# Two attentions that run all key groups over one half of the rows, then over the other

## What is computed

```
x = x + attn0(layernorm(x), ctx, ctx, mask)     # rope on q and k, softmax, @ wo
x = x + ffn0(layernorm(x))                      # 512 -> 1376 -> 512, rounded to int8 steps
x = x + attn1(layernorm(x), concat(ctx, x))     # rms norm on q and k, softmax, @ Wo
x = x + ffn1(layernorm(x))                      # int8 fake quantisation, two 512 x 512 products
```

## Time and profile before

| | us |
|---|---|
| median of three runs | 1549.08 |
| the three runs | 1549.51, 1549.08, 1546.22 |
| the profiled execution, its own time | 1546.81 |
| span from its first to its last instruction | 1545.0 |

### The profile page before, as it was taken

The page is one execution under the profiler, slowest core; times in us unless marked ns, Lnnn a source line. Parts: engine busy times, 40 slices in busy tenths (PEclk is TensorE's granted clock), DMA queues, the critical chain, the costliest instruction groups (busy, mean ns, idle before and its releaser), DMA issues.

```text
span 1545.0 us, 28746 instructions
## 1 busy us (share of the span) xinstructions
PE 1481.8 (96%) x11536; PEld 1271.7 (82%) x11536; DVE 957.9 (62%) x1989; ACT 591.7 (38%) x1428; POOL 565.1 (37%) x468
## 2 busy tenths in 40 slices
PE   6899999999999998999899999999999999999985
PEld 5788888888888876887698899888889988888973
DVE  7655666666656667666866556455655645565588
ACT  4322132222213214442355353444435344443556
POOL 4535363444436324552134122222312222231248
PEclk9999999999999999999999999999999999999999
DMA  6111020101102003220102011010101001010201
GB/s 196 36 34 43 28 69 22 49 28 42 42 28 62 8 21 96 61 77 21 42 28 70 1 42 29 28 42 17 54 2 42 28 28 42 15 55 1 82 2 55
DMA packets 84302, 64.45 MB, mean 42 GB/s; under 512 B 7280, under 2 KB 71024, under 8 KB 84176
## 3 DMA queue, kind: packets, MB, share of 16 engines
q1 hardware_dynamic: 83600, 62.47, 14.0%
q10 hardware_dynamic: 576, 0.20, 0.0%
HBM read 60.56 MB, written 2.10 MB: 41 GB/s over the span
## 4 chain that ended last, share of the span: by engine, by line
PE 47%; DVE 2%; POOL 1%; issue 1%; ACT 0%; DVEq 0%; ACTq 0%; POOLq 0%
PE att_proj L70 35%; PE att_att L788 4%; PE att_sco L746 4%; PE att_att L763 2%; PE att_proj L710 1%; PE att_sco L725 1%; POOL ffn_y L468 0%; DVE ffn_top L420 0%; DVE ffn_y L462 0%; POOL x_rows L406 0%; DVE ffn_y L416 0%; PE att_att L234 0%; DVE stats L375 0%; DVE x_rows L1031 0%; ACT ffn_y L427 0%
## 5 line engine op out<-in xcount | busy, mean ns | idle before, releaser
L144 POOL TENSOR_TENSOR att_w_lo<-w_raw,att_w_hi 128x512 fp32r<-128x512 f32 x160 | 203.4, 1295 | 209.4 <-ACT att_w_hi L139 203.5
L1380 POOL TENSOR_TENSOR att_probs<-att_probs,att_total 128x512 f32<-128x512 f32 x64 | 82.8, 1294 | 461.4 <-DVE att_total L1015 344.9
L70 PE MATMUL att_proj<-att_w_hi,kv_hi 128*128 128x256 f32 x768 | 221.0, 288 | 10.7 <-DVE kv_lo L252 10.5
L70 PE MATMUL att_proj<-att_w_lo,kv_hi 128*128 128x256 f32 x768 | 216.3, 282 | 0.0
L70 PE MATMUL att_proj<-att_w_hi,kv_lo 128*128 128x256 f32 x768 | 216.1, 281 | 0.0
L70 PE MATMUL att_proj<-att_w_hi,att_o_hi 128*128 128x512 f32 x512 | 206.7, 404 | 5.1 <-issue 4.6
L70 PE MATMUL att_proj<-kv_hi,att_w_hi 128*128 128x512 f32 x512 | 208.9, 408 | 1.5 <-DVE kv_lo L243 1.5
L70 PE MATMUL att_proj<-kv_hi,att_w_lo 128*128 128x512 f32 x512 | 202.7, 396 | 0.0
L70 PE MATMUL att_proj<-kv_lo,att_w_hi 128*128 128x512 f32 x512 | 202.7, 396 | 0.0
L1031 DVE TENSOR_TENSOR x_rows<-att_proj,x_rows 128x512 f32<-128x512 f32 x128 | 88.4, 691 | 183.8 <-PE att_proj L70 183.7
L70 PE MATMUL att_proj<-att_w_lo,att_o_hi 128*128 128x512 f32 x512 | 201.6, 394 | 0.0
(11 more groups left out here) (165 smaller groups left out, 2855.4 us busy)
## 6 DMA issues: line engine op xcount, KB each, us to landing
w_raw<-in_wq SPq DMA_DIRECT2D x64, 256.0 KB, 3.0
w_raw<-in_wo SPq DMA_DIRECT2D x64, 256.0 KB, 2.8
w_raw<-in_wk SPq DMA_DIRECT2D x16, 256.0 KB, 3.3
w_raw<-in_wv SPq DMA_DIRECT2D x16, 256.0 KB, 3.2
w_raw<-in_gate_t SPq DMA_DIRECT2D x10, 256.0 KB, 3.0
w_raw<-in_up_t SPq DMA_DIRECT2D x10, 256.0 KB, 3.1
w_raw<-in_down_t SPq DMA_DIRECT2D x10, 256.0 KB, 3.0
spare<-in_ctx_t SPq DMA_DIRECT2D x4, 512.0 KB, 5.7
```

The lines of the kernel that those rows point to most:

```text
L70: ins = eng.matmul(out, a, b, start=(first and n == 0), stop=(last and n == 3 * len(terms) - 1))
L144: eng.tensor_tensor(self.lo[:, chunk], self.raw[:, n % RAW_SLOTS], raw(self.hi[:, chunk]), ALU.subtract)\
L1380: eng.tensor_tensor(probs[:, u % 2, 0:n], probs[:, u % 2, 0:n], total[:, u % 2, 0:n].unsqueeze(2).broadcast_to([P, n, KL]), ALU.mult)\
```

## The change

The order of the units is turned round. VISITS lists (g, h) with the half outside: all eight groups over rows 0 to 511, then all eight over rows 512 to 1023. A unit is now u = 2v + n, with visit v and head pair n. Each visit needs its ten chunks, so each chunk is loaded, rounded and split twice. The fillers become: visit 0's two units make the keys of visit 1; after that n = 0 projects the visit before, n = 1 makes the next visit's keys.

The late half is needed from visit 8 on. Its statistics move behind unit 1 of DVE (first attention), its row scales behind unit 2. One late tile each is normalised on DVE at the end of units 3, 5, 7 and 9, and transposed, rounded and split as an extra projection job in units 4, 6, 8 and 10 (LATE_X). The late context goes through the ring of raw slots, as four entries "ctx" of turns, in unit 5 (visit 2, LATE_CTX). The last visit's output chunks go into the query chunks' place.

```diff
+VISITS = [(g, h) for h in range(HALF) for g in range(NKV)]
+LATE_CTX = 2
+LATE_X = {4: 4, 6: 5, 8: 6, 10: 7}
...
-        for g in range(NKV):
-            self.turns += [(g, C_O + i) for i in range(GROUP)]
-            if g + 1 < NKV:
-                self.turns += [(g + 1, c) for c in (C_Q, C_Q + 1, C_K, C_V, C_Q + 2, C_Q + 3)]
+        self.turns += [(1, c) for c in (C_K, C_V, C_Q, C_Q + 1)]
+        for v in range(len(VISITS)):
+            if v + 1 < len(VISITS):
+                self.turns += [(v + 1, c) for c in ((C_K, C_V) if v else ()) + (C_Q + 2, C_Q + 3)]
+            if v + 1 < len(VISITS):
+                self.turns += [(v, C_O + i) for i in range(GROUP)]
+            if v + 2 == len(VISITS):
+                self.turns += [(v + 1, C_O + i) for i in range(GROUP)]
+            if v == LATE_CTX:
+                self.turns += [("ctx", k) for k in range(KT)]
+            if v + 2 < len(VISITS):
+                self.turns += [(v + 2, C_Q), (v + 2, C_Q + 1)]
...
+        if visit == "ctx":
+            src = self.ctx[:, chunk, BANK:2 * BANK]
...
-        if g == 0 and n < 2:
-            return keys(0, 1)[KVH // 2 * n:KVH // 2 * (n + 1)]
+        if v == 0:
+            return keys(1)[KVH // 2 * n:KVH // 2 * (n + 1)]
         if n == 0:
-            return outs(g - 1, 1)
...
+            return [("out", v - 1, t) for t in range(4)]
+        return keys(v + 1) if v + 1 < len(VISITS) else []
...
                 fill_rest(work)
+                if u in LATE_X:
+                    x_job(LATE_X[u])
                 q_job(u + 2, 0)
...
+                if u in LATE_X:
+                    lower_late(LATE_X[u])
                 q_refine(u + 1)
                 take_q(u + 2, 0)
                 take_q(u + 2, 1)
                 out_low(u)
...
+                if u == 1 and rope:
+                    for t in range(4, NT):
+                        first_stats(t)
+                if u == 2:
+                    scale_rows(eng, st, chain, intake.stage, 1)
+                if u + 1 in LATE_X:
+                    normalise_late(LATE_X[u + 1])
...
-                if n == 2:
-                    round_w(g + 1, C_K, C_V, C_Q + 2, C_Q + 3)
+                if n == 0 and v < LAST:
+                    round_w(v + 1, *((C_K, C_V) if v else ()), C_Q + 2, C_Q + 3)
+                if n == 1:
+                    round_w(v, *range(C_O, C_O + GROUP))
+                if n == 1 and v == LATE_CTX:
+                    round_w("ctx", *range(KT))
+                if u in LATE_X:
+                    round_late(LATE_X[u])
                 copy_turned(u)
...
+                if n == 1 and v + 2 <= LAST:
+                    round_w(v + 2, C_Q, C_Q + 1)
+                if u == UNITS - 3:
+                    eng.wait_ge(proj_full, proj_job["q", UNITS - 1, 1] + 1)
+                    round_w(LAST, *range(C_O, C_O + GROUP))
...
+                if n == 0 and 0 < v < LAST:
+                    split_w(v + 1, C_K, C_V)
+                if n == 1:
+                    split_w(v, *range(C_O, C_O + GROUP))
                 rotate("q", u + 2, 0)
...
                 rotate("q", u + 2, 1)
...
+                if n == 1 and v == LATE_CTX:
+                    split_w("ctx", *range(KT))
+                if n == 1 and v + 2 <= LAST:
+                    split_w(v + 2, C_Q, C_Q + 1)
```

More of the change, by code:

```diff
@@ L220, in normalise @@
                           ALU.subtract, ALU.mult).then_inc(self.xn_done[t // 4], 1)
-    def normalise_late(self, eng, t):
-        st, ring = self.st, len(self.xn)
-        eng.wait_ge(st.rows_scaled, HALF * self.stage + t // 4 + 1)
-        need(eng, self.turned, t - ring + 1)
-        eng.activation(self.xn[t % ring], st.x[:, t], ACT.Identity, bias=st.shift[:, t:t + 1], scale=st.rstd[:, t:t + 1])\
-           .then_inc(self.xn_done[t // 4], 1)
     def turn(self, eng, t):
@@ L529, in attention @@
     for u in range(UNITS):
-        g, n = divmod(u, 4)
-        for i, what in enumerate(filling(g, n)):
+        for i, what in enumerate(filling(u)):
             number(*what)
@@ L543, in attention @@
             number("row", 0)
-        number("out", NKV - 1, 1, t)
+        number("out", LAST, t)
     if tail:
@@ L712, in q_sums, with x_job, turn_keys @@
                 last.then_inc(proj_full, 1)
-            def turn_keys(g, h):
-                need(eng, sco_drained, SJ * key_unit(g, h))
-                if g == 0 and h == 0:
+            def x_job(t):
+                job = proj_job["x", t]
+                eng.wait_ge(intake.xn_done[1], t - 3)
+                room(eng, job)
+                for k in range(KT):
+                    last = eng.transpose(proj[job % 4][:, k * P:(k + 1) * P], xn_late[:, k * P:(k + 1) * P], st.ident[:])
+                last.then_inc(proj_full, 1)
+            def turn_keys(v):
+                need(eng, sco_drained, SJ * 2 * v)
+                if v == 0:
                     eng.wait_ge(intake.x_split, 4)
@@ L839, in _ @@
                     intake.turn(eng, t)
-                for j in range(3):
-                    kv_job(0, 0, j)
-                intake.turn(eng, 4)
-                intake.turn(eng, 5)
-                kv_job(0, 0, 3)
+                for j in range(KVH):
+                    kv_job(0, j)
                 q_job(0, 0)
-                intake.turn(eng, 6)
-                intake.turn(eng, 7)
                 q_job(0, 1)
-                turn_keys(0, 0)
+                turn_keys(0)
                 q_job(1, 0)
@@ L1026, in out_low, with add_out @@
                        .then_inc(out_drained, 1)
-            def add_out(g, h, t):
-                job, row = proj_job["out", g, h, t], 4 * h + t
+            def add_out(v, t):
+                g, h = VISITS[v]
+                job, row = proj_job["out", v, t], 4 * h + t
                 eng.wait_ge(proj_full, job + 1)
@@ L1063, in _ @@
                     intake.lower_x(eng, t)
-                for t in range(4, NT):
-                    first_stats(t)
                 eng.wait_ge(tables_landed, 64)
                 for j in range(KVH):
-                    take(("kv", 0, 0, j))
-                scale_rows(eng, st, chain, 0, 1)
+                    take(("kv", 0, j))
                 take_q(0, 0)
@@ L1072, in _ @@
                 take_q(1, 0)
-                for t in range(4, NT):
-                    intake.lower_x(eng, t)
                 eng.wait_ge(mask_landed, 32)
@@ L1177, in _, with round_w, copy_v @@
         def _(eng):
-            def round_w(g, *chunks):
-                if g == NKV:
-                    return
+            def round_w(v, *chunks):
                 for chunk in chunks:
-                    weights.round_chunk(eng, weights.turn_of[g, chunk])
-            def copy_v(g, h, j):
-                job, half, pair = proj_job["kv", g, h, j], 2 * g + h, tile_of(h, j)
+                    weights.round_chunk(eng, weights.turn_of[v, chunk])
+            def copy_v(half, j):
+                job, pair = proj_job["kv", half, j], tile_of(half % 2, j)
                 bank = proj[job % 4][:].rearrange("p (b w d) -> p b w d", b=2, w=2)
@@ L1408, in _ @@
                 intake.lower_ctx(eng, 3)
-                eng.wait_ge(st.rows_scaled, 6)
-                split_w(0, C_Q, C_Q + 1)
-                split_w(0, C_Q + 2, C_Q + 3)
-                scale_keys(0, 0)
-                for t in range(4, NT):
-                    intake.lower_ctx(eng, t)
+                split_w(0, *range(C_Q, C_Q + GROUP))
+                scale_keys(0)
+                split_w(1, C_K, C_V)
+                split_w(1, C_Q, C_Q + 1)
             for u in range(UNITS - 2):
-                g, n = divmod(u, 4)
-                work = [what for what in filling(g, n) if what[0] == "kv"]
+                v, n = divmod(u, 2)
+                work = [what for what in filling(u) if what[0] == "kv"]
                 for what in work[:-1]:
@@ L1761, in build @@
         st.consts, st.qk_ready = st.sem("consts"), st.sem("qk_ready")
-        st.ctx_landed = [st.sem(f"ctx_landed{i}") for i in range(4)]
+        st.ctx_landed = [st.sem(f"ctx_landed{i}") for i in range(2)]
         st.ctx_cols = a["ctx_t"].rearrange("(k p) t -> p k t", p=P)
```

371 lines of the change are left out of this document (172 added, 199 removed).

## The result

The changed kernel takes **1598.95 us** (median of 4 runs, 1596.32 to 1601.33) against 1548.28 us for the kernel before (4 runs), a ratio of 1.033 with a 95% interval of 1.0316 to 1.0344. The forecast was 1556 us with a range of 1542 to 1565. The direction was right. The size was not: about 9 us were forecast and 50 came.

The account below looks back on a forecast made before the run. PE, busy 96% of the span, was taken as the bound. Terms -6.0 - 3.2 - 0.7 + 2.0 + 4.9 + 8.9 + 3.0 = +8.9 gave 1555.7, or 1558.0 from the median; forecast 1556 us, range 1542 to 1565.

Parts of the forecast that it names:

- So the doubled streaming costs nothing: Both attentions: 80 more chunks each to load, round and split stay beside PE, within covers of 0.3 to 2 us.
- theory B: Follow-up expectation, second attention: POOL's later splits or weight loads come too late for PE's projections; early refinement leaves 1595 to 1601.
- by the slack of rows 6 and 7 nothing does: Doubled splits holding up DVE on PE's path: 128 us by the port-lock rule at 0.8 us each, nothing by profiled slack.
- Rival 2: POOL crowded in each of 14 later keys units, 1.1 us lost per unit: +15, so 1571; chance 0.08.
- Start of the first attention: Late transposes leave the start, units 0 and 1 wait less: net 6.4 us gained, 6.0 taken.
- The seven small waits: First attention, seven units' PE waits for POOL's normalisation, some 0.46 us each, go: 3.2 us gained.
- Row scales: Moved to the end of DVE's unit 2, delaying unit 3: 1.7 us lost in first attention, 0.3 in second.
- Late context: Unit 5: ACT's context rounding waits for ring and DMA, PE idles 4.9 us in first attention, 8.9 in second.
- 1.5 + 1.5 for the clock: Lower clock behind each of the two unit 5 stalls: 3.0 us lost together, bounds 0 and 5.
- End of the first attention: Idle of 2.75 us before the projection at 566.37 shrinks as that half no longer ends there: 0.7 us gained.
- Second attention, transposes that come back: Late transposes leave the second attention's start and come back in later units, 1.6 us each way: net 0.
- Last visit: Output chunks use the query slots, unit 30's exponentials come some 3 us later: cost 0, bound 1.

Follow-up runs that it names:

- the early chain: Changed kernel with VectorE's ten dependent query-scale refinement instructions moved, in the second attention, from each unit's end to just behind q_means: 1561.12 us.
- the pieces: Changed kernel with each of POOL's output splits in the second attention cut into four instructions of 128 columns, VectorE's order unchanged: 1564.87 us.
- the chain last: Changed kernel with VectorE's query-scale refinement moved, in the second attention, behind the query-product copies and output remainder, last in its unit: 1564.26 us.
- the kernel before with the early chain: Kernel before the change, with VectorE's query-scale refinement moved to just behind q_means in the second attention: 1551.80 us, ratio 1.0029.
- the last kernel but one: Changed kernel, refinement early except second attention's units 0 and 1, context rounding behind output rounding, first attention's row scales inside unit 2: 1541.14 us.

## Why the forecast failed

**The step that failed is "So the doubled streaming costs nothing".** It was argued with care for what PE wants of POOL (the normalisation, the splits themselves) and of ScalarE (four more roundings), and those covers held: theory B fell, and the thirteen other keys units from 3 to 29 lost nothing. What the step left out is VectorE. It placed the four output splits of the second attention at 914.28 to 919.3, "ahead of the projection", and did not ask what VectorE does in just that stretch. It runs the chain. The trace of before had the sign. In its unit 5 two links of the chain took 1.02 and 0.96 us beside the key scaling of the earlier trace rows and the other eight 0.17. In its unit 6, where four splits run, three links took 1.2 us each (VectorE, then POOL):

```profile
932.12 1.21 DVE L164 TENSOR_TENSOR att_q_tmp<-att_q_rms 128x8 f32<-128x8 f32 x1
933.36 1.20 DVE L165 SCALAR_TENSOR_TENSOR att_q_tmp<-att_q_tmp,att_q_mean 128x8 f32<-128x8 f32 x1
934.60 1.23 DVE L166 SCALAR_TENSOR_TENSOR att_q_rms<-att_q_tmp,att_q_rms 128x8 f32<-128x8 f32 x1
```

```profile
930.77 5.03 POOL L144 TENSOR_TENSOR att_w_lo<-w_raw,att_w_hi 128x512 fp32r<-128x512 f32 x4
```

That chain took 5.2 us and PE didn't wait, so no list of waits showed it. In the keys units of the changed kernel mostly five or six splits follow the key scaling, and the chain starts with the scaling: some 7 us more than 2, with the two things that PE's projections need queued behind. The term is 0 in the sum and measured 37.1 us (by the medians of the runs: 37.8 with the early chain, 34.1 with the pieces).

**The sentence "by the slack of rows 6 and 7 nothing does"** is the same error. The rule beside it was the right one: the Trainium skill (SBUF — State Buffer, section SBUF: two separate sides) gives the lock between VectorE and POOL for the whole instruction. It also says, which I left out, that VectorE takes part in it only in a two-port mode or with two SBUF inputs. The trace agrees: L984 and L1040, with an operand in a bank, keep their 0.69 us, and the links with two SBUF inputs are held up. L188 has a single input, in SBUF, and was held up too (0.66 us with the chain last); in which mode it ran no run shows. I took 0.8 us per split from the earlier trace rows, one instruction held up once. A dependent chain is held up once for each link: the links start 1.23 us apart beside splits of 1.24 us (6.21 for five), so each arrives when the next POOL instruction has begun.

**Rival 2** (POOL crowded in every keys unit) came nearest, but it looked for POOL being late, in the first attention, and priced 1.1 us a unit. POOL was in time and made VectorE late, in the second.

The other terms, one by one:

- Start of the first attention: -6.0 with unit 2 at -8.0 before the transposes come back. Measured -7.3 at unit 2. PE waits 1.3 us in unit 0 (forecast 1.4), and the clock behind it is 1.00 where it was 0.79. The transposes come back with 2.0 us (forecast 1.6). Right.
- The seven small waits, -3.2: the units 9, 13 and so on to 29 take 14.52 us instead of 15.15, 0.6 us less each in six units; the seventh wait, of unit 5, is covered by the stall. Right.
- Row scales, 1.7 + 0.3: unit 3 of the first attention is 1.4 us longer (1.19 of it a wait for the normalisation), that of the second not at all. Right within the bounds.
- Late context, 4.9 + 8.9, with 1.5 + 1.5 for the clock: unit 5 is 5.3 and 9.95 us longer and unit 6 of the first attention loses 1.3 us at clock 0.77. The run that moved the rounding gave 15.3 us for all of it, forecast 16.8. Right, and by the mechanism described. Only where PE meets it in the second attention is another place: the wait of 8.02 us stands at the weighting, not at the next scores:

```profile
914.58 2.19 ACT L154 ACTIVATE att_w_hi<-w_raw 128x512 fp32r<-128x512 f32 x4
924.31 0.63 ACT L154 ACTIVATE kv_hi<-w_raw 128x512 fp32r<-128x512 f32 x1 [7.54 <-DMA w_raw<-in_ctx_t]
...
928.64 1.06 ACT L1257 ACTIVATE att_probs_t<-att_att 128x512 f32<-128x512 f32 x2
```

These are ScalarE's rows of unit 5 in the second attention: it stands 7.54 us for the context, and the copy of the turned probabilities, for which PE waits 8.02 us, stands behind it.

- End of the first attention, -0.7: the idle of the earlier trace rows is now 2.12 us instead of 2.75. Right.
- At unit 31 of the first attention the terms summed to -1.1, and -1.1 was measured. From there to the second attention's first scores the changed kernel lost 1.75 us (236.81 against 235.07) where -0.7, and -1.6 for the second attention's transposes that leave, were forecast. The clock differs: 0.95 in this stretch, 0.97 before. At equal clock the new order is the shorter one: at 0.95 the kernel before with the early chain took 238.29 us, the changed kernel 236.81; at 0.97 the kernel before took 235.07, the last kernel but one above 233.51. So some 1.5 us of the forecast 2.3 were there, hidden by the clock, as far as single executions tell. Why the clock differs stays open.
- Second attention, transposes that come back: forecast 1.6, measured 0.44 in each of four units, 1.8.
- Last visit, 0: unit 30 is 1.9 us longer, outside the bound of 1. It is the chain there too, since it is 8.22 us again with the early chain.

**Clock.** Of the 47.5 us by which the steady part of the second attention grew (713.28 against 665.81), 33.1 are idle time of PE and 14.4 are more busy time for nearly the same matmuls. Little of that is clock. Three stretches of the changed kernel: 10.2 us at the stall of unit 5, then unit 8, in which PE waits 2.27 us, and unit 12, in which it waits 2.32 and 0.15:

```profile
924.10:934.34 10.24, 4.98 (x23) 5.01 (x24) 7.16 (x8) 7.30 (x14) 5.90 (x5) 0.50 0.57 175
979.17:1005.73 26.56, 24.29 (x183) 19.82 (x181) 18.72 (x34) 10.93 (x29) 11.05 (x9) 0.94 0.33 97
1076.23:1101.24 25.01, 22.54 (x178) 18.30 (x177) 18.51 (x32) 10.34 (x28) 11.15 (x9) 1.00 0.34 103
```

The lower level (0.50) is granted at the stall and for 3.4 us each behind the waits of units 8, 20 and 22 (2.27, 2.31 and 2.27 us). The other eleven units of the fourteen stay at 1.00, with waits of up to 2.39 us. What sets the three apart no run shows. An estimate from these rows: half of 3 x 3.4 us is 5.1 us of lower clock, and half of the 5.0 us in which PE worked at the stall is 2.5. The late transposes are 1.8. The rest, some 5 us, was lost at full clock: each of the eleven units is 0.46 to 0.49 us longer than its waits and transposes explain. In a run of matmuls one of 0.39 us starts every 0.23 us, and the first behind a wait takes 0.47, which I read as the overlap of neighbours, lost at each stop. With the chain early the clock is at 1.00 from 960 to 1460 us.

## What to carry to other kernels

When a change gives POOL more instructions on SBUF, look at what VectorE runs in the same stretch, not only at who waits for POOL. A chain of small dependent instructions between SBUF tiles costs one whole POOL instruction for each link, and whatever is queued behind the chain pays, once the chain is longer than what PE's queue covers (here some 7 us; one of 5.2 cost nothing). Cures that were measured here: run the chain where POOL is idle, or make POOL's instructions shorter. Here the engine whose busy time rose by much more than its instructions account for was being held up, and the page showed that in its first lines, not in the list of waits. And before a load is rounded by an engine that has other work, ask how long it stands there if its DMA waits for a ring.

## What was not expected of the hardware

- A 128x8 VectorE instruction between SBUF tiles: 0.17 us alone, 0.38 us beside POOL instructions of 0.42 us, 1.2 us beside those of 1.25, 0.17 again beside those of 0.22. VectorE's 128x512 instructions with an operand in an accumulator bank: 0.69 us in the same stretch as the 1.2.
- Cutting a POOL subtraction of 128x512 (1.24 us, five in 6.21, in unit 9) into four made it 1.68 us (4 x 0.42) when nothing else was changed, and 34 us were won by it, since only what VectorE waited for mattered.
- Fourteen waits of PE of 0.2 to 2.4 us, one every 48 us or so: the granted clock fell behind three of them, of 2.3 us, and stayed at 1.00 behind the others, some of which were as long.
